# Transformer layer with selective writes on one core: another order for the writes of the first four tiles

## What is computed

```python
def rat_write(res, y, wod_w, wab_w, wab_b, du_w, du_b):
    o_d = y @ wod_w.T                       # 512 outputs and 8 low-rank columns
    A_B = y @ wab_w.T + wab_b               # 112 gate columns
    delta = softplus(delta_low @ du_w.T + du_b)
    A_neg = -softplus(A_logit)
    A_bar = exp(delta * A_neg)
    B_bar = (A_bar - 1.0) / (A_neg - SSM_EPS) * B_proj
    B_bar_skip = delta * B_skip
    return hs * A_full + out * B_full
```

## Time and profile before

| what | value |
|---|---|
| median of 3 runs | 1874.6 us (1873.32 to 1875.7) |
| the profiled execution | 1875.35 us, span 1873.6 us |
| TensorE busy | 1652.1 us (88%) |
| VectorE busy | 1171.3 us (63%) |
| ScalarE busy | 794.4 us (42%) |
| GpSimd busy | 268.7 us (14%) |
| mean granted TensorE clock | 0.934 |

### The profile page before, as it was taken

One profiled execution on the slowest core, in us unless ns is written; L12 is line 12 of the kernel. 1 busy time (PEld: TensorE's weight loads), 2 busy tenths in 40 slices (PEclk: granted clock), 3 DMA queues, 4 the chain that ended last, 5 costly groups with the idle time before them and its releaser, 6 DMA issues.

```text
span 1873.6 us, 23597 instructions
## 1 busy us (share of the span) xinstructions
PE 1652.1 (88%) x8854; PEld 1141.1 (61%) x8854; DVE 1171.3 (63%) x1873; ACT 794.4 (42%) x1486; POOL 268.7 (14%) x243
## 2 busy tenths in 40 slices
PE   6799998799999956799898999887999998999866
PEld 5565655466666635677565677555677565775544
DVE  6678754688888847344347548547458455555576
ACT  1333235588888725344323444223444322341221
POOL 1235432423340000200002000003000002000000
PEclk7899999899999976699898999998999999999987
DMA  7367568588885152476464665554566544655711
GB/s 298 114 262 254 199 172 238 153 214 238 224 231 125 49 208 90 150 243 215 155 201 155 218 219 199 177 177 149 185 230 212 191 164 148 223 194 172 253 76 68
DMA packets 117221, 348.69 MB, mean 186 GB/s; under 512 B 16226, under 2 KB 33250, under 8 KB 101876
## 3 DMA queue, kind: packets, MB, share of 16 engines
q1 hardware_dynamic: 117108, 347.19, 57.3%
HBM read 271.37 MB, written 75.76 MB: 185 GB/s over the span
## 4 chain that ended last, share of the span: by engine, by line
PE 62%; DVE 22%; ACT 5%; issue 5%; DMA 3%; SPq 2%; POOL 1%; DVEq 0%; ACTq 0%; POOLq 0%
PE ps L1363 15%; PE ps L1375 11%; PE ps L396 4%; PE ps L818 4%; PE ps L1278 4%; PE ps L841 4%; PE ps L805 4%; PE ps L1321 3%; PE ps L1263 3%; PE ps L1306 3%; PE ps L1333 2%; ACT a_p L920 2%; SPq L141 2%; DVE m_A L1436 2%; PE ps L369 2%
## 5 line engine op out<-in xcount | busy, mean ns | idle before, releaser
L1363 PE MATMUL ps<-m_yhi,m_win 128*128 128x512 f32 x1024 | 352.8, 413 | 0.8 <-DMA m_win<-mlp_in_split 0.8
L1375 PE MATMUL ps<-m_wod,m_hT 128*128 128x512 f32 (+1 forms) x1024 | 308.6, 450 | 8.0 <-DVE m_hT L1561 8.0
L1375 PEld LDWEIGHTS ps<-m_wod,m_hT 128*128 128x128 f32 x1024 | 171.8, 199 | 150.1 <-issue 149.7
L1363 PEld LDWEIGHTS ps<-m_yhi,m_win 128*128 128x128 f32 x1024 | 195.4, 191 | 50.1 <-issue 4.9
L862 DVE TENSOR_REDUCE a_negmax<-ps 128x1 f32<-128x640 f32 (+7 forms) x176 | 180.7, 1027 | 63.5 <-PE ps L808 62.7
L920 ACT ACTIVATE a_p<-ps,a_negmax 128x128 f32<-128x128 f32 (+7 forms) x256 | 188.8, 751 | 43.1 <-DVE a_negmax L862 41.0
L1363 PE MATMUL ps<-m_ylo,m_win 128*128 128x512 f32 x512 | 204.0, 398 | 0.0
L818 PE MATMUL ps<-ident,a_p 128*128 128x128 f32 x1152 | 157.9, 276 | 16.1 <-DVE a_pT L875 15.9
L1593 ACT ACTIVATE m_turned<-ps 128x512 f32<-128x512 f32 x128 | 74.1, 593 | 190.2 <-PE ps L1263 190.2
L805 PE MATMUL ps<-a_k,a_q 128*128 128x512 f32 (+3 forms) x384 | 124.5, 403 | 16.6 <-ACT a_p L920 14.7
L818 PEld LDWEIGHTS ps<-ident,a_p 128*128 128x128 f32 x1152 | 123.8, 142 | 18.2 <-DVE a_pT L875 16.8
(11 more groups left out here) (202 smaller groups left out, 2737.7 us busy)
## 6 DMA issues: line engine op xcount, KB each, us to landing
m_win<-mlp_in_split SPq DMA_DIRECT2D x128, 512.0 KB, 4.3
m_wod<-in_wod2T SPq DMA_DIRECT2D x128, 316.0 KB, 3.1
m_wod<-in_wod1T SPq DMA_DIRECT2D x64, 316.0 KB, 3.1
p_xT<-in_xT SPq DMA_DIRECT2D x16, 1024.0 KB, 8.9
p_x<-in_x SPq DMA_DIRECT2D x16, 1024.0 KB, 10.4
a_q<-qk_split SPq DMA_DIRECT2D x64, 256.0 KB, 6.5
a_k<-qk_split SPq DMA_DIRECT2D x128, 128.0 KB, 7.1
mlp_in_split<-a_w_two SPq DMA_DIRECT2D x32, 512.0 KB, 3.4
```

The lines of the kernel that those rows point to most:

```text
L1363: m = nc.tensor.matmul(bank_of("m", blk, step), win[s][:, wl, ic, :], y[:, k, :], start=(ic == 0 and p3 == 0), stop=(ic == HCH - 1 and p3 ...
L1375: m = nc.tensor.matmul(ps[:, b, 0:cn], hT[:, k, P * q:P * q + P], w2[s][:, c0:c0 + cn], start=(k == 0), stop=(k == MCH - 1))
```

## The change

The table of positions for the first four tiles gets other values, and tiles stand four positions apart and not three. Nothing else is edited.

```diff
-        FIRST_AT = [("loado", None, -100), ("load", None, -99.9), ("wod", None, 0), ("low", None, 1),
-                    ("delta", None, 2), ("gates", None, 3), ("scale", None, 4), ("sum", None, 5), ("turn", 0, 6),
-                    ("turn", 1, 6.5), ("read", 0, 7), ("turn", 2, 7), ("read", 1, 7.5), ("turn", 3, 7.5),
-                    ("read", 2, 8), ("read", 3, 8.5), ("stats", None, 9), ("norm", None, 10)]
+
+        FIRST_AT = [("loado", None, -100), ("load", None, -99.9), ("wod", None, -2), ("low", None, .5),
+                    ("delta", None, 1), ("gates", None, 2), ("scale", None, 6.5), ("sum", None, 7),
+                    ("turn", 0, 9), ("turn", 1, 9.2), ("read", 0, 9.4), ("turn", 2, 9.6), ("read", 1, 9.8),
+                    ("turn", 3, 10.4), ("read", 2, 10.6), ("read", 3, 10.8), ("stats", None, 11.2), ("norm", None, 12)]
...
-                placed += [(-200 + 3 * i + at, ("a", i, part, q)) for part, q, at in FIRST_AT]
+                placed += [(-200 + 4 * i + at, ("a", i, part, q)) for part, q, at in FIRST_AT]
```

## The result

The changed kernel takes 1891.28 us (median, 1890.6 to 1891.97) against 1875.15 us before: a ratio of 1.0088 with a 95% interval of 1.007 to 1.0105, 16.1 us slower. The forecast was 1894.2 with a range of 1885 to 1899.

What follows compares the result with a forecast made beforehand. TensorE bounds the whole span, but between attention and the first feed-forward block no engine is full and queue order counts. Terms 6.7 + 5.7 + 1.1 + 2.9 + 3.2 = +19.6 us on 1874.6 give 1894.2, range 1885 to 1899.

Steps and rivals of the forecast that it cites:

- Tile 0: Between tile 1's products and tile 0's sum: scaling queued behind later tiles' work, sum 6.7 us later.
- Tile 1: Step from sum 0 to sum 1: VectorE waits for tile 3's late products, 26.6 us against 20.9, 5.7 more.
- my signs of being wrong: Trace signs against the forecast: tile 3's products ending before 712, high clock after 720, or sum 3 before 765.
- Tile 2: Step from sum 1 to sum 2: statistics, norm and quarters stand ahead, 22.3 us against 21.2, 1.1 more.
- Tile 3: Step from sum 2 to sum 3: scaling behind norm and four quarters, 21.7 us against 18.8, 2.9 more.
- Tail: Sum 3 to block 0's first transposes: norm 2 ahead of quarter 0, 17.5 us against 14.3, 3.2 more.
- The other queues: SyncE's loads and stores and GpSimd's order: loads move but nothing is late; delay reaches the end undiminished, 0 us.
- The clock rule: TensorE's idle gaps between bursts bring back the half clock: first transposes at 789.2, without the rule 780.8.
- (b): Rival: the clock stays high through the stretch between attention and first feed-forward block, +11 us, 1886; chance 8%.
- (c): Rival: the delay is mostly absorbed behind 769.6, total within 0.2% of before; chance 3%.
- Rival (a): Edit works as its order suggests: from sum 0 on VectorE never waits, -11.5 us, 1863; chance 4%.

Runs made afterwards that it cites:

- e1: Changed kernel with turn 3 moved to 10.55 and norm to 13.25, behind quarter 1 of the next tile: 1877.5 us against 1873.61 before, ratio 1.0021.
- e8: Kernel before with gates moved to 2.8 and scale to 2.9, ahead of the next products' copy: 1859.32 us against 1873.55, ratio 0.992.
- e4: Kernel before with products, low, delta and gates placed ahead of the previous tile's scale and sum: 1875.5 us against 1873.37, ratio 1.0009.
- e9: Changed kernel with scale ahead of the next products and norm behind quarter 1: 1867.44 us against 1873.37 before, ratio 0.9967.
- e7: Changed kernel with 9 idle products ahead of low of tiles 2 and 3: 1888.04 us against 1873.55 before, ratio 1.008.
- b2: Kernel before with the first four tiles' order written out piece by piece, without early scaling: 1855.89 us against 1873.55, ratio 0.9902.
- e5: Kernel before with only statistics at 8.6 and norm at 8.7, ahead of the next tile's turns: 1877.0 us against 1873.55, ratio 1.002.
- e6: Changed kernel with 20 idle products ahead of low of tiles 2 and 3: one execution took 1901.07 us.

## Why the prediction was right, point by point

Direction, mechanism and place held: e1 and e8 move the places that I named, and both come out as the timetable has them, within 1 us in each step. The whole kernel lost 16.1 us for the 19.6 forecast.

- **Tile 0, 6.7 us later**: 6.5 measured (17.56 against 11.04); the scaling starts at 689.40, and with the 1.0 us by which this execution was ahead that is 690.4 for the 690.6 forecast. I had named the gates and the products of the later tiles together; e4 and e9 show that the gates alone make 6.1 to 6.3 of it.
- **Tile 1, 5.7 more**: 2.2. This is the term that was mis-sized, and it makes up the whole difference of 3.6 us between forecast and result in the stretch. I had TensorE at the low clock until 713, since the clock of the kernel before rose only within a tile's products. In the changed kernel it rose within 704 to 706, behind transposes, the delta product and reads and before any of tile 3's products. These began 0.9 us sooner than forecast, set beside the same start, and took 4.4 us for 7.3 (of which 0.2 is a slip: 3 x 2.0 + 1.1 is 7.1), and VectorE waited 3.26 us before L1413 for the 6.7 forecast. Of my signs of being wrong, products ending before 712, the high clock after 720 and sum 3 before 765, the first was at its limit: they end at 711.4, or 712.4 with the 1.0 us, for the 716.1 forecast. The other two did not come. e7 shows the price of the low clock that was left in that step, 1.3 us.
- **Tile 2, 1.1 more**: 1.0. **Tile 3, 2.9 more**: 2.8, with 9.17 us before L1460 for the 9.0 forecast. **Tail, 3.2 more**: 3.5.
- **The other queues** cost nothing, and nothing was absorbed later: 15.9 us in the stretch, 16.1 in the kernel.
- **The clock rule**: the value by the Trainium skill's rule ("TensorE: Matmul & The Clock Gate", "Why this matters for your kernels") was 789.2 for the first transposes and 780.8 without it. Measured is 784.55, or 785.6 with the 1.0 us by which this execution was ahead. The gaps did take the clock down (0.50 in the windows from 692 to 700 and from 716 to 722), as the Trainium skill says; after the first it came back sooner than I had it.
- **Rivals (b) and (c)** did not come: the clock was at 0.50 from 692 to 704 and from 716 on, and nothing of the loss was absorbed.
- **Rival (a)**, VectorE never waiting at -11.5 us, was refuted for this change. (Its third step was added up 0.2 us short: 14.0 and 1.9 are 15.9.) Its mechanism is real, though: b2 is that case, with -17.7, and e8 has -14.2 with two positions. I had named the condition, ScalarE's scaling done before VectorE asks, but gave the places of norm and quarter 3, which decide 12 of 16 us beside early products and gates, only as two terms of 2.9 and 3.2; that moving them back would bring tile 3 below its old step I saw only when I worked out e1.

## What to carry to other kernels

Where several engines walk one hand-written list, an item placed early on one engine is placed ahead of something on every engine. Ask for each engine what the moved piece now stands in front of, and whether that one is due sooner. A piece that the next long item waits for (here scale, for VectorE's sum) belongs ahead of pieces that are needed only later (the copy of the next products; e8, -14.2 us), and a piece that has to wait for a late result (norm, for the statistics) belongs behind those that are ready (e1, e5). A timetable of the stretch, worked out from durations of one trace and checked against the old order first, gave such steps to within 1 us each but for those in which the clock came out otherwise (tile 1 of the change, the tails of e4, e9 and b2) and those with idle products.

## What the runs showed that I had not expected

TensorE's clock rose within 704 to 706 us in the changed kernel, where TensorE had done four transposes, a delta product, transposes and reads since 699.96 and none of a tile's products. From 726.05 to 737.4 it was busy without a gap with a delta product, transposes and reads, and stayed at 0.50. What tells the two apart stays open. Nor does the order of a stretch fix the level. The tail of e4 is that of the kernel before, transposes and reads in the same order, and its first four rows last as long as before's; then the clock rises within 762 to 764 and the tail takes 12.7 us at 0.63 on the mean, against 14.3 at 0.50. The tails of e9 and b2 ran at 0.84 and 0.64 and took 11.2 and 12.7 us. The others with norm behind quarter 1 took 14.3 at 0.50, and those with norm ahead of quarter 0 took 17.8 at 0.50. And one idle product of 128x512 in f32 shows as two records of 0.43 us at the high clock, 0.87 us in all, which made e6 outlast its wait.
